# Second FFN's gelu block moved from slot 7.5 to slot 10.5, second products and GpSimd's first product with C moved along

## The reference, cut to what matters

```
x = x + 0.5 * ffn(layernorm(x))        # "f1"
x = x + mamba(layernorm(x))            # "p", with its own residual
x = x + 0.5 * ffn(layernorm(x))        # "f2", same weights as f1
ffn:   idx = argmax(softmax(x @ Wg + bg))                     # 8 experts
       h = gelu(einsum('th,ehi->tei', x, W1) + b1); y = einsum('tei,eih->teh', h, W2) + b2
       take y[idx]
mamba: xn = rmsnorm(x) * w; x_path, z = split(xn @ in_proj.T)
       x_path = silu(causal_conv4(x_path)); dt_x, B, C = split(x_path @ x_proj.T)
       dt = softplus(dt_x @ dt_proj.T + b)
       h = exp(dt * A) * h + (dt * x) * B    # a scan over 256 steps, 16 states a channel
       y = sum_n(h * C) + D * x; out = (y * silu(z)) @ out_proj.T + residual
```

## Time and profile before

| what | value |
| --- | --- |
| median of 3 runs | 1492.56 us (1492.42 to 1492.58) |
| profiled execution, its own time | 1495.2 us |
| its span, first to last instruction | 1493.4 us |
| mean granted TensorE clock | 0.849 |
| busy: TensorE matmul / VectorE / ScalarE / GpSimd | 1232.2 / 1061.7 / 874.2 / 1067.6 us |
| one iteration with all stages | 82.41 us |

### The profile page before, as it was taken

How to read it: one execution, slowest core, us unless ns; L and a number is a source line. 1 busy time by engine, 2 the same in 40 slices (tenths; PEclk the granted TensorE clock), 3 DMA queues, 4 the chain that set the end, 5 groups by cost and what they waited for, 6 DMA issues and landing times.

```text
span 1493.4 us, 16302 instructions
## 1 busy us (share of the span) xinstructions
PE 1232.2 (83%) x5188; PEld 612.7 (41%) x5188; DVE 1061.7 (71%) x1713; ACT 874.2 (59%) x1171; POOL 1067.6 (71%) x900
## 2 busy tenths in 40 slices
PE   2777768889898989989898988899898978667677
PEld 1333314234443534445353444444353434333344
DVE  2022887887878787877878787878878776979910
ACT  0244656476666767575667667575756675474532
POOL 1026796978878788868788787878687886997600
PEclk9989876788888998888888889888888987978786
DMA  3005050413233231503232332305032322232000
GB/s 84 1 0 205 10 198 9 158 43 120 92 108 106 89 111 33 181 23 127 80 120 92 108 106 73 127 24 185 28 115 85 122 85 105 101 114 92 1 7 14
DMA packets 60405, 130.02 MB, mean 87 GB/s; under 512 B 7744, under 2 KB 26864, under 8 KB 52128
## 3 DMA queue, kind: packets, MB, share of 16 engines
q1 hardware_dynamic: 60320, 128.98, 25.1%
HBM read 106.94 MB, written 22.02 MB: 86 GB/s over the span
## 4 chain that ended last, share of the span: by engine, by line
PE 41%; ACT 24%; DVE 23%; issue 8%; POOL 3%; SPq 1%; ACTq 0%; DVEq 0%; DMA 0%; POOLq 0%
PE PH L462 12%; PE PY L477 9%; DVE dA L759 9%; PE G L451 9%; ACT hs L610 6%; ACT dA L632 5%; DVE hb L757 4%; ACT hs L597 4%; DVE hb L763 3%; PE PH L461 3%; ACT L614 3%; ACT L610 2%; PE Y L489 2%; PE G L511 2%; PE G L531 2%
## 5 line engine op out<-in xcount | busy, mean ns | idle before, releaser
L936 POOL TENSOR_TENSOR hb<-dtx_rep,bs 128x1024 f32<-128x1024 f32 x256 | 598.8, 2361 | 0.0
L759 DVE TENSOR_TENSOR_SCAN dA<-dA,hb 128x512 f32<-128x512 f32 x352 | 429.8, 1221 | 68.5 <-ACT dA L632 61.6
L632 ACT ACTIVATE dA<-dt_rep,A 128x512 f32<-128x512 f32 x512 | 342.2, 689 | 143.4 <-DVE hb L763 128.7
L597 ACT COPY hs<-PH 128x512 f32<-128x512 f32 x256 | 149.4, 584 | 388.2 <-PE PH L462 387.9
L462 PE MATMUL PH<-xnT,W 128*128 128x512 f32 x512 | 339.0, 749 | 0.0
L477 PEld LDWEIGHTS PY<-W,hs 128*128 128x128 f32 x2048 | 281.8, 208 | 101.2 <-issue 88.8
L477 PE MATMUL PY<-W,hs 128*128 128x128 f32 x2048 | 323.2, 304 | 0.0
L944 POOL TENSOR_TENSOR hb<-hb,cs 128x1024 f32<-128x1024 f32 x80 | 188.4, 2355 | 140.7 <-DVE hb L757 140.7
L763 DVE TENSOR_TENSOR hb<-dA,cs 128x512 f32<-128x512 f32 x352 | 243.5, 692 | 25.2 <-DVE dA L759 0.9
L757 DVE TENSOR_TENSOR_SCAN hb<-dA,hb 128x512 f32<-128x512 f32 x160 | 186.3, 1206 | 102.6 <-ACT dA L632 99.5
L489 PE MATMUL Y<-hb,Sel 128*32 128x512 f32 x1024 | 164.5, 716 | 19.8 <-POOL hb L944 10.4
(11 more groups left out here) (85 smaller groups left out, 1190.7 us busy)
## 6 DMA issues: line engine op xcount, KB each, us to landing
dtx_rep<-dtx_rows SPq DMA_DIRECT2D x32, 1024.0 KB, 6.5
dt_rep<-dt_rows SPq DMA_DIRECT2D x32, 1024.0 KB, 8.2
bs<-bc_rows SPq DMA_DIRECT2D x64, 256.0 KB, 3.7
cs<-bc_rows SPq DMA_DIRECT2D x64, 256.0 KB, 4.5
dtx_rows<-dtx SPq DMA_DIRECT2D x32, 256.0 KB, 2.5
dt_rows<-dt SPq DMA_DIRECT2D x32, 256.0 KB, 2.6
X<-in_x SPq DMA_DIRECT2D x16, 256.0 KB, 3.0
out<-X SPq DMA_DIRECT2D x16, 256.0 KB, 2.4
```

What stands on the lines that cost most here:

```text
L597: nc.scalar.copy(hs[:, w, e, :], PH[:, :]).then_inc(ph_free, 1)
L632: nc.scalar.activation(dA[u % NA][:, :], dt_rep[:, h, g, :], ACT.Exp, scale=A[:, h, g, q:q + 1]).then_inc(decay, 1)
L759: nc.vector.tensor_tensor_scan(a, a, x_in_hb, 0.0, ALU.mult, ALU.add).then_inc(scan, 1)
L936: nc.gpsimd.tensor_tensor(hb[:, s % HR], dtx_rep[:, h, 2 * m:2 * m + 2, :], bs[:, q, None, :].broadcast_to([P, 2, CH]), ALU.mult).then_inc ...
```

## The change

The tables at the head change, and nothing else. The second FFN's gelu block moves from slot 7.5 to slot 10.5 of ScalarE. Its second products move from slots 10 to 15 to slots 12 to 15 and, for experts 4 to 7, to slots 0 and 1 of the next iteration. VectorE's addition of them and the store of the output move one slot back. The first FFN's first products and copies end in slot 14 instead of 15, one copy (expert 3) sits between the halves of the moved block, and the copy of expert 0, which sat in the block, stands at the head of slot 8. The first FFN's second products begin one slot later. On TensorE z1 stands ahead of the state sum of slot 3, the second FFN's product e6 ahead of `out`, bc and e7 in slot 5, and dt1 and dt0 one behind the other in slot 6. GpSimd's first product with C belongs to slot 2 instead of slot 1.

```diff
-STAGES = [("ln_f1", 3, 0, 1, 0), ("gate_f1", 3, 1, 2, 1), ("z0", 1, 0, 2, 2), ("z1", 1, 1, 3, 2),
-          ("out", -1, 0, 4, 1), ("oh_f1", 3, 1, 5, 1), ("bc", 1, 0, 6, 0), ("dt1", 1, 1, 6, 1),
-          ("dt0", 1, 0, 7, 0), ("ln_f2", -1, 1, 9, 0), ("gate_f2", -1, 0, 10, 1), ("oh_f2", -1, 1, 12, 0),
+STAGES = [("ln_f1", 3, 0, 1, 0), ("gate_f1", 3, 1, 2, 1), ("z0", 1, 0, 2, 2), ("z1", 1, 1, 3, 1),
+          ("out", -1, 0, 4, 1), ("oh_f1", 3, 1, 5, 1), ("bc", 1, 0, 5, 0), ("dt1", 1, 1, 6, 0),
+          ("dt0", 1, 0, 6, 1), ("ln_f2", -1, 1, 9, 0), ("gate_f2", -1, 0, 10, 1), ("oh_f2", -1, 1, 12, 0),
...
-ACT_AT = {"ln_f1": 1.5, "silu": 4.0, "bc": 6.0, "dt1": 6.5, "dt0": 7.0, "soft": 7.0, "gelu_f2": 7.5,
+ACT_AT = {"ln_f1": 1.5, "silu": 4.0, "bc": 5.5, "dt1": 6.5, "dt0": 6.5, "soft": 7.0, "gelu_f2": 10.5,
...
-DVE_AT = {"gated1": 1.5, "y_f2": 1.5, "gate_f1": 3.0, "out": 4.5, "oh_f1": 6.0, "stats_f2": 5.0, "gated0": 9.5,
+DVE_AT = {"gated1": 1.5, "y_f2": 2.5, "gate_f1": 3.0, "out": 4.5, "oh_f1": 6.0, "stats_f2": 5.0, "gated0": 9.5,
...
-SP_AT = {"x_out": 3, "x_in": 4, "bc": 6, "b0": 8, "dt": 9, "b1": 10, "c0": 10, "b2": 12, "c1": 12, "b3": 14, "dtx1": 14,
+SP_AT = {"x_out": 4, "x_in": 4, "bc": 6, "b0": 8, "dt": 9, "b1": 10, "c0": 10, "b2": 12, "c1": 12, "b3": 14, "dtx1": 14,
...
-W1_AT = [[(8, 2, 7, 3, 3), (9, 2, 9, 0, 3), *[(s, 0, s, 0, 3) for s in (10, 11, 12, 13, 14, 15)]],
-         [(15, 1, 15, 0, -1), (15, 2, 15, 1, -1), (15, 3, 15, 3, -1), (1, 0, 0, 0, -2), (2, 0, 2, 0, -2),
-          (3, 0, 3, 0, -2), (5, 0, 4, 2, -2), (6, 0, 6, 0, -2)]]
-
-W2_AT = [[(s, 1, 2) for s in (4, 6, 8, 8, 8, 9, 9, 9)],
-         [(s, k, -2) for s, k in ((10, 1), (11, 1), (12, 1), (13, 1), (14, 1), (14, 1), (15, 1), (15, 2))]]
+W1_AT = [[(8, 2, 8, 0, 3), (9, 2, 9, 0, 3), (10, 0, 10, 0, 3), (10, 2, 10, 3, 3),
+          *[(s, 0, s, 0, 3) for s in (11, 12, 13, 14)]],
+         [(15, 0, 15, 0, -1), (15, 1, 15, 1, -1), (15, 2, 15, 3, -1), (1, 0, 0, 0, -2), (2, 0, 2, 0, -2),
+          (3, 0, 3, 0, -2), (4, 0, 4, 0, -2), (5, 0, 6, 0, -2)]]
+
+W2_AT = [[(s, 1, 2) for s in (5, 7, 7, 8, 8, 8, 9, 9)],
+         [(12, 1, -2), (13, 1, -2), (14, 1, -2), (15, 2, -2), (0, 1, -3), (0, 1, -3), (1, 1, -3), (1, 1, -3)]]
...
-POOL_C = (1, 3, 5, 9, 14)
+POOL_C = (2, 3, 5, 9, 14)
```

## The result

| what | before | after |
| --- | --- | --- |
| median | 1494.58 us (17 runs) | 1498.54 us (17 runs) |
| profiled execution, own time / span | 1495.2 / 1493.4 us | 1499.68 / 1497.9 us |
| mean granted TensorE clock | 0.849 | 0.876 |
| busy: TensorE / VectorE / ScalarE / GpSimd | 1232.2 / 1061.7 / 874.2 / 1067.6 us | 1197.9 / 1062.9 / 869.5 / 1065.4 us |

The ratio after to before is 1.0026, 95% interval 1.0013 to 1.0038: slower by about 4 us, where +16.9 was forecast. Lines of the changed kernel stand one number higher than those of before.

The account below looks back on a forecast made before the run. No engine alone was the bound, but the order in which they release each other. Terms -3.3 + 3.0 + 1.3 + 0.7 = +1.7 us in 12 iterations (+20.4), -4.5 and +1 gave +16.9: 1509 us, range 1464 to 1534.

Parts of the forecast that it names:

- e6: Second FFN's product for expert 6, moved ahead of `out` into its wait: 1.4 us off the way to dt0.
- e1: First FFN's second product for expert 1, moved behind dt0: 0.89 us off the way from `out` to dt0.
- One of my own signs of being wrong: Distance of two softplus blocks under 82 us; near 84 was forecast.
- The gelu block leaves slot 7.5: VectorE's 4.23 us wait before slot 9 goes; 1.8 us an iteration are left won at slot 10.
- The block at 10.5 at nothing: VectorE's work from slot 10 to 12 covers ScalarE's moved block with 1.0 us to spare; costed at nothing.
- (a): TensorE starved 2.8 us beside the moved block, then half clock: +3.0 us an iteration, bounds 0 and +5.3.
- (b): Turn of the iteration: TensorE starved 3.0 us before the second FFN's product for expert 2; +1.3 us, bounds 0 and +3.7.
- Slots 4 to 7: TensorE's reordered products bring dt0, the softplus and slot 8 1.5 us earlier in each iteration.
- (c): Slots 2 to 5: a slow stretch ending later makes e6 and `out` pay; +0.7 us an iteration, bounds 0 and +2.6.
- The last iterations: Last three scan iterations win half of three waits, -4.5 us; the block behind xnT at the end costs +1.
- The clock falls but costs little: Rival: dense products bring the clock back early, (a) 1.1, (b) 0.6, (c) nothing; 1470 us, chance 0.26.
- the first rival: The clock holds, so (a) to (c) are zero: 1449 us, chance 0.08.

Follow-up runs that it names:

- bg_fill_warm: Kernel before with the gelu block's move alone, tables of before in iterations -4 to -1, and 3 zero matmuls in each of two starved places: ratio 0.9712.
- bg_pool: Kernel before with the gelu block's move alone, and GpSimd's first product with C in slot 2: ratio 0.9862 to the kernel before.
- b_gelu: Kernel before with only the second FFN's gelu block moved and what goes with it: ratio 0.9900 to the kernel before.
- a_e0: Changed kernel with only the first FFN's second product e0 back in slot 4: ratio 0.9985 to the kernel before.
- a_pool1: Changed kernel with GpSimd's first product with C back in slot 1: ratio 1.0109 to the kernel before.
- bg_w2: Kernel before with the gelu block's move alone, and the first FFN's second products one slot later: ratio 1.0085 to the kernel before.
- a_w2: Changed kernel with all of the first FFN's second products in the slots of before: ratio 0.9991 to the kernel before.
- bg_stages: Kernel before with the gelu block's move alone, and z1, bc, dt1, dt0 in the places of the change: ratio 0.9988 to the kernel before.
- a_e0 with its matmuls: Changed kernel with second product e0 in slot 4 and 3 zero matmuls in each of the two starved places: ratio 0.9793 to the kernel before.

## Why the prediction was right or wrong

**The direction came out, for another reason.** Slower was forecast because the block's new place would cost more clock than it saves. The block alone is 1.0% faster. Added to it by themselves, the later second products of the first FFN (not priced, but for e1, which I had put down as a gain) and the order of the stages (a gain in the forecast) lose 1.9% and 0.9%. In the whole change no part carries the loss by itself: undoing the second products wins 0.35%, undoing the order of the stages wins nothing.

That 1498.5 us lies inside the stated range is luck. The iterations came out 9 x (1.7 + 0.5) = 20 us better than forecast, and the start lost 10.7 us for which there was no term. One of my own signs of being wrong came too: five of the nine distances between softplus blocks are under 82 us (81.76 to 81.88).

**The gelu block leaves slot 7.5: right, and to a tenth in this iteration.** Slot 9 was to start at dt0 + 9.1, slot 10 at dt0 + 13.9. In the iteration above dt0 ends at 840.88, by a row of the chain that ended last (start, length, what; the row below, 839.59 + 1.29); slot 9 starts at 850.07, dt0 + 9.2, and slot 10 at 854.86, dt0 + 14.0:

```profile
839.59 1.29 PE G L452 x3
```

**The block at 10.5 at nothing: right.** VectorE waits 0.21 us before slot 11, as before, and less than that before slot 12.

**(a) TensorE beside the block: the step that failed.** The gap was forecast well, its price not. I added 4.8 us of half clock and a late one-hot copy; +3.0 taken. From slot 10's scan to the convolution VectorE needs 879.88 - 854.86 = 25.0 us, against 789.69 - 765.47 = 24.2 before: **0.8** us, most of it a longer wait for the convolution's input (2.88 instead of 2.29). The one-hot copy in slot 13 waits less than 0.2 us. What was wrong is the length of the stretch: it lasts for one product and one sum, not for four pieces of work. The runs give the price by the length. From slot 10 to the convolution VectorE needs 24.2 us where the clock is held (bg_fill_warm), 24.7 with 3.4 us at half clock beside the block, mostly 25.0 to 25.5 with 6.8 (26.2 at most, in bg_pool), 25.5 to 26.1 with 10.2 and 27.4 with 13.7. The changed kernel has 3.4 or 6.8 in its nine full iterations; +3.0 is the price of 13.7. The old slow stretch from 766 to 776, in the same place, cost nothing there: before, the distance is 24.2 too.

**(b) The turn of the iteration: right place, half the size.** Slot 1 starts 895.94 - 879.88 = 16.1 us behind the convolution, against 805.03 - 789.69 = 15.3: **0.7** instead of 1.3. VectorE's wait grew by 0.73 us (3.15 to 3.88, where over 4 was forecast). Where the clock is held (bg_fill_warm) the distance is 15.3 again, and with 6.8 us at half clock (the long iterations of b_gelu) it is 17.3.

**Slots 4 to 7 and (c): wrong, -1.5 + 0.7 forecast, 0 measured.** From slot 1's scan to the end of dt0 both kernels take 27.1 us (805.03 to 832.17 in the rows of before; 895.94 to 923.08 in the chain after). The rows below are VectorE in those slots before:

```profile
789.69 2.72 DVE L776 SCALAR_TENSOR_TENSOR xs<-G,Wc,xs 128x506 f32<-128x506 f32 x4 [2.29 <-ACT xs L647]
...
805.03 2.34 DVE L757 TENSOR_TENSOR_SCAN hb<-dA,hb 128x512 f32<-128x512 f32 x2 [3.15 <-ACT dA L632]
```

I had seen that e1 goes behind dt0, and not that e0 goes from behind `out`, where it filled VectorE's addition, to ahead of dt1. Back in slot 4 (a_e0), e0 gives 1.3 us from slot 1 to slot 8. In b_gelu, which has e6 ahead of `out` and neither other part, that stretch is 1.2 us shorter than before (30.12 against 31.30), near the 1.4 that I gave e6.

Together: -1.7 + 0.8 + 0.7 + 0 = -0.2 us for the iteration traced, -0.5 in the mean of nine, against +1.7. The term that was mis-sized most is (a), by 2.2 us.

**The start: a missing term, +10.7 us.** The iterations ahead of the first scan stood in no step. With the tables of before in these four the loss is gone, and 11.4 us of span with it.

**The last iterations: near.** From chunk 13's softplus on the rest is 1.5 us shorter, where -4.5 + 1 was forecast. It is 4.8 us shorter up to chunk 15's softplus and 3.2 longer behind it; these were not traced further.

**The rivals.** "The clock falls but costs little" described the block correctly: the block alone ran at 0.9900, 1478 us, near its 1470. The rule of the Trainium skill that stood with the first rival, "TensorE: Matmul & The Clock Gate", section "HAM oscillation — how this bites in real kernels", would have the clock hold through such gaps; the trace disagrees again, with the clock lost right behind the gap of 3.13 us. The prediction's own reading of the trace of before on this point is not exact: it says that the gaps from 760 to 766 and from 800 to 804 were no longer than 1.96 us. They were 1.64 and 0.27 in the first, and 1.17 and 2.27 in the second, where the clock fell 1.3 us into the longer gap (at 803.5). What the clock is worth where it does hold the last runs show: 81.0 to 78.6 us an iteration.

**Why several kernels settle at 81.9 us.** VectorE's timelines cut an iteration into four pieces: from the scan of slot 1 to that of slot 8, to that of slot 10, to the convolution, and to the next scan of slot 1. "Slow" is the time at half clock beside the block, "wait" that of the one-hot copy in slot 13. All are of the iteration that scans chunk 10, but for those marked.

| kernel | 1 to 8 | 8 to 10 | 10 to convolution | to 1 | slow | wait |
| --- | --- | --- | --- | --- | --- | --- |
| before | 31.30 | 11.56 | 24.22 | 15.34 | 10.2 | 0 |
| changed | 31.27 | 9.83 | 24.72 | 16.05 | 3.4 | 0 |
| a_pool1 | 30.92 | 9.83 | 25.12 | 16.06 | 6.8 | 0.23 |
| bg_w2 | 30.63 | 9.83 | 25.43 | 16.04 | 6.8 | 0.52 |
| a_e0 | 29.99 | 9.83 | 26.09 | 16.01 | 10.2 | 1.18 |
| a_w2, bg_stages | 29.99 | 9.82 | 26.09 | 16.02 | 10.2 | 1.19 |
| b_gelu, chunk 9 | 30.12 | 8.93 | 24.67 | 16.01 | 3.4 | 0 |
| b_gelu | 30.12 | 8.93 | 27.38 | 17.34 | 13.6 | 2.47 |
| bg_fill_warm, chunk 7 | 30.12 | 8.94 | 24.23 | 15.27 | 0 | 0 |

What a kernel of the middle rows wins from slot 1 to slot 8 comes back from slot 10 to the convolution, as the slow stretch grows: 31.27 + 24.72, 30.92 + 25.12, 30.63 + 25.43 and 29.99 + 26.09 are 56.0 to 56.1 each. In bg_fill_warm, where the clock is held, 30.12 goes with 24.23. So it is the clock that takes the gains, as far as this pair and a_e0 with its matmuls show. Why the stretch grows by just so much, and why the rests of these kernels differ, stays open.
